# Flamingo gated cross-attention layer on one core: a second buffer for the softmax scales, the last V product moved forward, and the rows of maxima queued ahead of the last four of twelve group loads

## What is computed

```
x   = x + tanh(g_xattn) * Attention(LN(x), ctx, ctx)      # B=4, S=512, D=256, 16 heads of 16
x   = x + tanh(g_ffn)   * (MoE(LN(x)) + Shared(LN(x)))    # 8 experts, top 2, hidden 256; shared hidden 512

Attention: q,k,v = Q Wq'+bq, K Wk'+bk, V Wv'+bv;  softmax(q k'/4) v  per head;  times Wo' + bo
MoE:       router logits, top 2, softmax of the two; silu(proj)*gate @ fc2 for each chosen expert
Shared:    silu(h gate_w) * (h up_w) @ down_w
```

## Time and profile before

| | us |
|---|---|
| Median of 3 runs | 471.99 (471.62 to 473.8) |
| Profiled execution, its own time | 474.82 |
| Its span | 472.6 |
| Granted TensorE clock, mean | 0.964 of full |
| Busy: TensorE / VectorE / ScalarE / GpSimd | 440.2 / 315.0 / 267.2 / 223.1 |

### The profile page before, as it was taken

How to read it: one execution, slowest core, us unless ns; L and a number is a source line. 1 busy time by engine, 2 the same in 40 slices (tenths; PEclk the granted TensorE clock), 3 DMA queues, 4 the chain that set the end, 5 groups by cost and what they waited for, 6 DMA issues and landing times.

```text
span 472.6 us, 8388 instructions
## 1 busy us (share of the span) xinstructions
PE 440.2 (93%) x2294; PEld 225.8 (48%) x2294; DVE 315.0 (67%) x719; ACT 267.2 (57%) x564; POOL 223.1 (47%) x345
## 2 busy tenths in 40 slices
PE   8999999999969979495999999999999999999997
PEld 7654444333323323132355464575555555555745
DVE  1976938999866959394837877555665656542574
ACT  2545439999977959395864611113666667631110
POOL 5335525877863939384654476750333233322000
PEclk9999969999997989798999999999999999999999
DMA  8689561334362434327082582241323223211931
GB/s 259 242 238 295 172 234 53 90 97 106 84 115 64 89 89 82 76 65 144 19 242 86 157 289 91 101 121 49 90 81 91 83 88 91 81 56 48 359 112 60
DMA packets 45500, 58.93 MB, mean 125 GB/s; under 512 B 12496, under 2 KB 25680, under 8 KB 45456
## 3 DMA queue, kind: packets, MB, share of 16 engines
q1 hardware_dynamic: 38864, 46.05, 35.0%
q0 software_dynamic: 4960, 10.53, 7.1%
q10 hardware_dynamic: 1632, 1.84, 1.2%
HBM read 36.35 MB, written 19.81 MB: 119 GB/s over the span
## 4 chain that ended last, share of the span: by engine, by line
PE 64%; ACT 8%; DMA 8%; DVE 7%; issue 7%; SPq 6%; POOL 0%; ACTq 0%; DVEq 0%; POOLq 0%
PE PS L1665 11%; PE PS L1776 9%; ACT R L816 7%; PE PS L1500 6%; DMA QK<-mparts 6%; PE PS L1678 6%; PE PS L1621 5%; PE PS L1795 5%; PE PS L1440 4%; PE PS L1387 4%; PE PS L1771 3%; PE PS L1547 3%; SPq L397 2%; SPq L394 2%; PE PS L1790 2%
## 5 line engine op out<-in xcount | busy, mean ns | idle before, releaser
L939 DVE TENSOR_REDUCE nmax<-PS 128x2 f32<-128x1024 f32 x114 | 134.2, 1214 | 42.0 <-PE PS L1387 40.5
L816 ACT ACTIVATE R<-PS 128x512 f32<-128x512 f32 x256 | 134.3, 630 | 37.3 <-PE PS L1621 36.8
L1621 PE MATMUL PS<-QK 50*128 50x512 f32 x256 | 84.1, 475 | 22.5 <-DMA QK<-mparts 21.2
L679 POOL TENSOR_TENSOR R<-R 128x512 f32<-128x512 f32 x48 | 61.6, 1284 | 43.6 <-ACT R L802 42.0
L1621 PEld LDWEIGHTS PS<-QK 50*128 50x128 f32 x256 | 37.4, 197 | 83.4 <-ACT R L816 38.7
L1500 PE MATMUL PS<-R 128*32 128x512 f32 x512 | 72.6, 639 | 2.5 <-ACT R L816 1.6
L718 POOL DMA_INDIRECT token_y<-R,dest x34 | 32.6, 959 | 86.7 <-DVE R L1270 86.4
L1387 PE MATMUL PS<-QK 48*128 48x512 f32 x256 | 61.6, 458 | 1.3 <-DVE nmax L925 0.9
L1776 PE MATMUL PS<-R 128*128 x100 | 47.3, 595 | 0.2 <-ACT R L884 0.2
L831 ACT ACTIVATE R<-PS 128x512 f32<-128x512 f32 x16 | 9.6, 597 | 60.6 <-PE PS L1665 60.6
L802 ACT COPY R<-PS 128x512 f32<-128x512 f32 x64 | 38.6, 603 | 7.5 <-PE PS L1500 7.0
(11 more groups left out here) (181 smaller groups left out, 621.5 us busy)
## 6 DMA issues: line engine op xcount, KB each, us to landing
QK<-q_parts SPq DMA_DIRECT2D x96, 64.0 KB, 2.8
QK<-k_parts SPq DMA_DIRECT2D x96, 64.0 KB, 2.9
k_parts<-R SPq DMA_DIRECT2D x8, 512.0 KB, 4.0
q_parts<-R SPq DMA_DIRECT2D x8, 512.0 KB, 4.8
R<-in_fc_w_dram SPq DMA_DIRECT2D x16, 256.0 KB, 5.1
R<-token_y SPq DMA_DIRECT2D x4, 1024.0 KB, 9.1
R<-slot_x SPq DMA_DIRECT2D x25, 129.0 KB, 2.1
fc<-in_fc_w_dram SPq DMA_DIRECT2D x16, 128.0 KB
```

Source lines behind the costliest of these rows:

```text
L679: nc.gpsimd.tensor_tensor(OT[i % 2], OT[i % 2], PART[kt - 1], ALU.add).then_inc(summed, 1)
L816: nc.scalar.activation(PT[:, kt, j, :], PS[:, ring_bank("score", TB * i + kt, j), :], ACT.Exp).then_inc(exp_done, 1)
L939: nc.vector.tensor_reduce(nmax[:, i % 2, at:G * TB:G * TB // 2], PS[:, smax_bank(n):smax_bank(n) + 2, :], AX.X, ALU.max, negate=True).then ...
L1621: mm(PS[:, ring_bank("score", TB * i + kt, j), :], KST[g][at, h, kt * P:(kt + 1) * P], QS[g][at, h, :], start=True, stop=True).then_inc(st ...
```

## The change

- **Scales:** `SCALES` becomes a list of two tiles, the memory of `W["v"]` and that of `W["q"]`. Pair n uses tile n mod 2. `load_scale(i)` waits for the pair two before, not the pair before; the arrival semaphores are four instead of two; at i = 2 SyncE also waits until the q and k projections are done, the last readers of `W["q"]`. In GpSimd's loop `scale_context` moves ahead of `bias_x` and `add_part(i, 1)`.
- **Rows of maxima:** in SyncE's turn, pieces 4 and 5 of the group load (four of the twelve DMAs) move behind `load_max(i + 1)`.
- **V:** in steps 0 and 1 of group 0 the first four products for V go ahead of the first pair of `scores_for_max`, and ScalarE's `v_copy` goes ahead of the fourth exponential.

```diff
-        SCALES = W["v"][:, :, :].rearrange("p c d -> p (c d)")
+        SCALES = [W[n][:, :, :].rearrange("p c d -> p (c d)") for n in "vq"]
...
-        scale_ready, scale_in, ctx_scaled = sem("scale_ready"), sems("scale_in", 2), sem("ctx_scaled")
+        scale_ready, scale_in, ctx_scaled = sem("scale_ready"), sems("scale_in", 4), sem("ctx_scaled")
...
-                wait(sp, ctx_scaled, i // 2)
-                sp.dma_start(SCALES[64 * (i % 2):64 * (i % 2 + 1), :],
-                             r_scr[i].unsqueeze(1).to_broadcast([G, DK, S])).then_inc(scale_in[i % 2], 16)
+                if i == 2:
+                    sp.wait_ge(qk_done, 4 * B)
+                wait(sp, ctx_scaled, i // 2 - 1)
+                sp.dma_start(SCALES[i // 2 % 2][64 * (i % 2):64 * (i % 2 + 1), :],
+                             r_scr[i].unsqueeze(1).to_broadcast([G, DK, S])).then_inc(scale_in[i % 4], 16)
...
                     sp.wait_ge(exp_done, G * (TB * i + 1))
-                    load_group(i + 3, range(2, UNIT))
+                    load_group(i + 3, (2, 3))
                 if i + 1 < GROUPS:
                     load_max(i + 1)
+                if 0 < i and i + 3 < GROUPS:
+                    load_group(i + 3, (4, 5))
...
-                    pool.wait_ge(scale_in[h], 16 * (n + 1))
-                nc.gpsimd.tensor_tensor(CTX[:, n, :], CTX[:, n, :], SCALES, ALU.mult).then_inc(ctx_scaled, 1)
+                    pool.wait_ge(scale_in[2 * (n % 2) + h], 16 * (n // 2 + 1))
+                nc.gpsimd.tensor_tensor(CTX[:, n, :], CTX[:, n, :], SCALES[n % 2], ALU.mult).then_inc(ctx_scaled, 1)
...
+                if i >= 5 and i % 2:
+                    scale_context((i - 5) // 2)
                 if i < 12:
                     bias_x(range(4 + i, 5 + i))
                 add_part(i, 1)
-                if i >= 5 and i % 2:
-                    scale_context((i - 5) // 2)
...
                     for j in range(G):
+                        if i == 0 and kt < 2 and j == 3:
+                            v_copy(B - 1, PS[:, ring_bank("v", kt), :], kt)
...
-                    if i == 0 and kt < 2:
-                        v_copy(B - 1, PS[:, ring_bank("v", kt), :], kt)
...
                     scores(kt, 0)
                     scores(kt, 1)
+                    if i == 0 and kt < 2:
+                        last_value_rows(kt, 0)
                     for n in pairs[0:1]:
                         scores_for_max(n)
                         scores_for_max(n + 1)
-                    if i == 0 and kt < 2:
-                        last_value_rows(kt, 0)
```

## The result

| | before | after |
|---|---|---|
| Median of 6 runs | 470.9 (468.99 to 473.8) | 447.13 (445.28 to 448.29) |
| Ratio, with 95% interval | | 0.9488 (0.945 to 0.9526) |
| Profiled execution, its own time | 474.82 | 445.28 |
| Its span | 472.6 | 443.0 |

The change made the kernel 5.1% faster, 23.8 us in the medians. 441.2 was forecast, with 437 to 457 as the range.

A forecast was written before the change was run, and what follows sets the result against it. Late rows of maxima, after SyncE's wait for GpSimd's scaling bunched loads, were taken to stretch every second attention group. Gains of 26.0 (groups) and 4.8 us (V), 30.8 together, from 471.99 gave 441.2 us, range 437 to 457.

The forecast's parts named there:

- the prediction's own signs: Attention groups: forecast wrong if a group at full clock takes over 10.5 us or the clock falls anywhere within attention.
- The sum: Whole kernel: 26.0 us from attention groups 1 to 13 plus 4.8 from V, 30.8; nothing from group 14 on.
- I take the gain from the median: Final step: subtract 30.8 us from the median 471.99, not the profiled 474.82, giving 441.2 us.
- the 27.3 us of excess: Groups 1 to 13: 157.3 us against 130, the excess from late maxima in every second group.
- behind a queue that was filled without a pause: Turn 5's maxima: issued 0.96 us late after twelve group loads, landing 6.59 us after the second one's issue.
- The second rival: Maxima still land late every second group behind the broadcast load; 454 us if half the excess stays, 467 if all; 11%.
- its "against": Attention: every turn has the broadcast load ahead, and turn 4's maxima landed in time behind it.
- the packs and loads had drained: While TensorE waited in attention: 67 GB/s at DMA share 0.33 read as a few engines working, the rest idle.
- the sentence on the rule: Maxima and broadcast load share few DMA engines; the change leaves the broadcast in front, 5.8 us ahead instead of 6.2.
- rival 1: Attention groups: last four loads about 1.2 us late in each, groups 11.15 us, total 455 us; chance 16%.
- V: right: Group 0: gaps filled save 1.5 us, avoided clock fall more; group 1 starts at 71.7, gain 4.8 us.
- Rivals 4 and 5: Attention: late pieces 4 and 5 lower the clock, 483 us, 4%; or another SyncE wait leaves 470 to 473, 3%.

The follow-up runs named there:

- part 4: Changed kernel rerun unaltered on another chip beside the kernel before (482.94 us): 456.12 us, ratio 0.9453.
- without the order: Changed kernel with all twelve group loads again ahead of the rows of maxima, second buffer and V kept: 442.26 us, 0.9406 of before.
- changed, small broadcast: Changed kernel with the 128 KB broadcast load of scales replaced by 8 KB, most scales not loaded: 456.01 us, 0.9475 of before.
- four DMAs of 16 rows: Kernel before with each broadcast load of the scales cut into four 16-row DMAs, same bytes: 465.8 us, 0.9926 of before.

## Why the prediction was right, and where it wasn't

- **The number was right, the mechanism in part.** By the prediction's own signs the forecast is wrong: three groups at a full clock took over 10.5 us, and in the execution of part 4 the clock fell within attention. Most of the stall did go with the buffer, but for a reason of which the prediction had only half.
- **The sum held for the traces.** 30.8 us were forecast and the two spans differ by 29.6: V 4.8 for 4.8, the groups 24.7 for 26.0, the end 0.1 for 0.
- **The step that was off is the last of the sum**, "I take the gain from the median". The profiled execution of before, 474.82, is the slowest of its seven, and that after the fastest of its own (445.28). The medians differ by 23.8. Of the 5.9 us between 441.2 and 447.13, 2.8 are this step (474.82 - 30.8 would be 444.0), 1.3 the sum (445.28), and 1.9 that the profiled execution after was a fast one. Executions of the kernel before went from 467.81 to 478.24 on one chip, at mean clocks from 0.974 to 0.953. That points to an excess that differs from one to the next, but only one of them has a trace. If so, 2.8 us above the median was a sign that the 27.3 us of excess were on the high side. The result is within the range, but neither this nor the cost of the order was foreseen: the range was wide enough because of other rivals.
- **The second buffer: right in size, incomplete in cause.** The wait did bunch the loads, and with the buffer alone the groups are 9.9 to 10.2. But "behind a queue that was filled without a pause" is not enough: twelve loads without a pause and with a small load ahead of them let group 7 start 3.6 us after the maxima's issue, with the four-row broadcast ahead 7.2. The second rival had this mechanism, and its "against" was the mistake: in turn 4 the maxima came 7.7 us behind the broadcast load and not 6.2, and the group loads between them took 2.5 us to land (median of the k loads), not 4.3. The buffer does two things at once: it takes the late issue away and sends the broadcast load off sooner, to 7.5 to 8.0 us before the maxima. The order alone, with the maxima on time at distances of 4.4 to 4.7 and groups of 11.2 to 12.1, shows that the second counts by itself.
- **A row misread.** (67 GB/s from 138 to 140) was taken as a time in which "the packs and loads had drained". They hadn't: the last group load, issued at 134.95, landed at 141.5. It was the tail of this very backlog.
- **The order: a term with the wrong sign.** It stood in the sum as robustness against late issues and 0.2 us a group. It shortens the distance from the broadcast load from some 7.7 to some 5.8 us, and with it three groups in one execution and six in another were 0.4 to 1.4 us longer. The prediction gave this very distance, 5.8, in the sentence on the rule, and put it into the second rival at 11%. With that rule of the Trainium skill ("DMA: Bandwidth & Descriptors", "Rules for kernel authors": an outermost dimension below 16 confines a DMA to at most that many engines) the trace agrees: the broadcast load has four completions there and each copy of the maxima two, and with 16 rows outermost in each of four DMAs the loads behind it were not delayed.
- **The last four loads (rival 1) were not late.** TensorE's idle time before `scores_for_max` is put down to a DMA of k once, 0.4 us in all, and that before group 1.
- **V: right.** The clock stays full and group 1 starts at 71.69, forecast 71.7. V alone moved the median by 3.9 us (0.9936), and 4.3 on top of the second buffer. That the clock falls after those idle times is so in four of five traces only, so 4.8 is again the size for one trace.
- **Rivals 4 and 5** (slower; nothing) have nothing for them in any run.

The distances in one view, from broadcast issue to maxima issue and from there to the next group's start:

| Kernel, turn | Broadcast to maxima | Maxima to start |
|---|---|---|
| before, 4 | 7.73 | 3.22 |
| before, 6 | 6.23 | 7.23 |
| order only, long group | 4.52 | 5.28 |
| changed, group 8 | 5.87 | 4.49 |
| without the order, group 5 | 7.91 | 3.31 |
| without the order, group 6 | 7.74 | 3.65 |
| changed, small broadcast, group 8 | 5.92 | 3.07 |
| four DMAs of 16 rows, group 6 | 7.95 from the first, 6.66 from the last | 2.41 |

The distance is no sharp rule: in the changed kernel group 10 has 5.90 and then 3.16 us, beside group 8's 5.87 and 4.49. What stays open is why 5.8 us does harm in some groups and not in others, three in one execution and six in another; the views give the share of all 16 DMA engines together and not of the few that matter. With twelve loads between, at a distance of 6.2 (before, turn 6), it is worse than with eight at 4.5 (order only), so group loads add to the backlog; by how much each wasn't measured.

## What to carry to other kernels

When a small DMA that an engine waits for lands late, ask not only how full the queue is but what is in front of it on the DMA engines that it uses. Look for a narrow broadcast there, measure the time from its issue to that of the small one, and how long the loads between them take to land. Then change that time or the broadcast's shape before the order of the wide loads. Test each part of a change on the others: here two parts mended the same stall, one by itself gave 14 us and cost 4 to 5 where the other was in place. And where a stall varies from run to run, don't take its size from one trace.

## What the hardware showed that wasn't expected

- The broadcast load of 128 KB (four heads outermost) needs 4.2 to 6.7 us from its issue in the kernel before, and the group loads issued behind it in turn 5 take 4.3 us to land where they take 2.7 behind a load of 8 KB. Behind the same bytes as four DMAs of 16 rows they take 2.6, and such a DMA of 32 KB itself 1.8.
- Two idle times of TensorE, 0.91 and 1.16 us, with 3.7 us of work between them, were followed by the fall of the clock to 1.2 GHz in four traces of five, and in the fifth, with the same two, they weren't. With the first gap filled and the second left, the clock stayed full in its one trace.
- The same kernel differed by 11 to 13 us between chips (470.09 and 471.81 against 482.94 for the kernel before), while the changed kernel's ratio to it was 0.9488 and 0.9453.
